# Four transposes of quantized codes as 16 bit halves, one hidden row per bank, and new step tables, in a chained four layer kernel on one Trainium2 core

## What is computed

```python
def _act_quant(x):
    scale = 127.0 / clip(max(abs(x), axis=-1), 1e-05)
    return clip(round(x * scale), -128, 127) / scale
def _bitlinear(x, w, nw):            # w is ternary times a scale
    xn = x * rsqrt(mean(square(x)) + 1e-08) * nw
    return act_quant(xn) @ weight_quant(w).T
# layer 0, for each element
mx = layernorm(x) * (1 + sc_msa) + s_msa
i, f, g = bitlinear(mx, wi), sigmoid(bitlinear(mx, wf)), bitlinear(mx, wg)
o = scan over tokens: h = f * h + silu(i) * (1 - f)
x = x + g_msa * bitlinear(rmsnorm(o) * silu(g), wo)
m = layernorm(x) * (1 + sc_mlp) + s_mlp
x = x + g_mlp * bitlinear(silu(gate) * y, wm2)    # gate, y = bitlinear(m, wm1)
# layer 1, for each element: a pre map, a fold over four tokens, a merge map,
# and y = gelu(h @ ffn_w1 + b) @ ffn_w2 + x with a hidden width of 1024
```

## Time and profile before

| what | value |
|---|---|
| timed runs, median (lowest to highest of 3) | 2154.37 us (2153.43 to 2154.45) |
| the profiled execution's own time | 2156.48 us |
| its span, first to last instruction | 2154.3 us |
| busy PE, DVE, ACT, POOL | 1839.9, 1328.7, 1121.0, 568.9 us |
| mean granted TensorE clock | 0.913 |

### The profile page before, as it was taken

The page is one execution under the profiler, slowest core; times in us unless marked ns, Lnnn a source line. Parts: engine busy times, 40 slices in busy tenths (PEclk is TensorE's granted clock), DMA queues, the critical chain, the costliest instruction groups (busy, mean ns, idle before and its releaser), DMA issues. The chain is left out here.

```text
span 2154.3 us, 26196 instructions
## 1 busy us (share of the span) xinstructions
PE 1839.9 (85%) x8728; PEld 1104.3 (51%) x8744; DVE 1328.7 (62%) x2922; ACT 1121.0 (52%) x2127; POOL 568.9 (26%) x775
## 2 busy tenths in 40 slices
PE   2355779999999996589899999999999856899998
PEld 1133557677766674133454545454544445567666
DVE  5757698878876516668786868677774114332331
ACT  6556588888776521046756575666666400221221
POOL 0256565567445213000010101010101100323322
PEclk9656699999999997589999999999999977999999
DMA  9400000000000003220203021111200020000000
GB/s 373 127 33 8 18 18 1 18 18 14 1 13 11 3 1 98 52 59 5 63 3 64 7 59 26 40 34 32 53 14 3 6 96 1 3 18 10 20 10 20
DMA packets 88312, 78.20 MB, mean 36 GB/s; under 512 B 9969, under 2 KB 82123, under 8 KB 87923
## 3 DMA queue, kind: packets, MB, share of 16 engines
q1 hardware_dynamic: 88080, 76.50, 12.9%
q10 hardware_dynamic: 98, 0.03, 0.0%
HBM read 46.67 MB, written 4.27 MB: 24 GB/s over the span
## 5 line engine op out<-in xcount | busy, mean ns | idle before, releaser
L1896 DVE TENSOR_REDUCE l_small<-l_psum 128x1 f32<-128x512 f32 x512 | 329.5, 684 | 137.2 <-PE l_psum L1843 132.3
L1655 ACT ACTIVATE l_prob<-l_psum 128x512 f32<-128x512 f32 x512 | 286.4, 596 | 230.0 <-PE l_psum L1713 226.7
L1843 PE MATMUL l_psum<-l_kT,l_qT 96*128 96x512 bf16 x512 | 192.2, 412 | 27.1 <-DMA l_kT<-l_early 12.1
L1713 PE MATMUL l_psum<-l_qT,l_kT 99*128 99x512 bf16 x512 | 175.6, 388 | 16.0 <-ACT l_prob L1655 14.3
L1639 POOL TENSOR_TENSOR k_x_res<-k_x_res,l_add 128x256 f32<-128x256 f32 x32 | 23.3, 727 | 469.9 <-DVE l_add L1940 469.9
L1722 PE MATMUL l_psum<-l_prob,l_v 128*32 128x512 f32 x1024 | 138.1, 612 | 0.2
L1843 PEld LDWEIGHTS l_psum<-l_kT,l_qT 96*128 96x128 bf16 x512 | 49.6, 98 | 171.1 <-DVE l_small L1896 117.9
L1787 PE MATMUL l_psum<-l_w,l_gu 128*128 128x256 f32 x512 | 134.8, 392 | 0.7 <-ACT l_gu L1671 0.7
L94 PE MATMUL l_psum<-l_hT,l_w_f 128*128 128x512 f32 x256 | 120.0, 597 | 5.7 <-ACT l_gu L1013 5.7
L94 PE MATMUL l_psum<-l_hT,l_w 128*128 128x512 f32 x256 | 116.8, 606 | 8.6 <-ACT l_hT L2250 8.6
L94 PE MATMUL l_psum<-l_turned_over,l_w 128*128 128x512 f32 x256 | 120.5, 597 | 4.2 <-ACT l_gu L1671 4.2
(11 more groups left out here) (389 smaller groups left out, 3891.5 us busy)
## 6 DMA issues: line engine op xcount, KB each, us to landing
su_raw<-in_L_cond_wa SPq DMA_DIRECT2D x6, 1536.0 KB, 21.9
l_qT<-l_early SPq DMA_DIRECT2D x32, 192.0 KB, 3.6
l_kT<-l_early SPq DMA_DIRECT2D x32, 192.0 KB, 3.3
k_x_res<-in_x SPq DMA_DIRECT2D x1, 4096.0 KB
l_w<-in_L_cond_W SPq DMA_DIRECT2D x4, 1024.0 KB, 12.5
l_qT<-l_early SPq DMA_DIRECT2D x32, 128.0 KB, 3.1
l_kT<-l_early SPq DMA_DIRECT2D x32, 128.0 KB, 3.0
out<-k_x_res SPq DMA_DIRECT2D x8, 512.0 KB, 2.9
```

The lines of the kernel that those rows point to most:

```text
L1655: act.activation(prob[:, s % 2, j, :], psum[:, 2 + n % 2, :], ACT.Exp, scale=float(HD) ** -0.5).then_inc(exp_ready.sem, 1)
L1713: pe.matmul(psum[:, 2 + n % 2, :], kT[e % 2][:, head, tok(s % T)], qT[e % 2][:, head, :], start=True, stop=True).then_inc(st_ready.sem, 1)
L1843: pe.matmul(psum[:, n % 2, :], qT[e % 2][0:SROWS, n // T, tok(n % T)], kT[e % 2][0:SROWS, n // T, :], start=True, stop=True).then_inc(s_re ...
L1896: dve.tensor_reduce(mx[:, n % T, n // T:n // T + 1], psum[:, n % 2, :], AX.X, ALU.max).then_inc(max_ready.sem, 1)
```

## The change

The code is now made with bias ROUND + CODE, CODE = 16384.0. The low 16 bits of the f32 word are then 16384 plus the code. `low(a)` views an f32 tile as bf16 and takes every second element, the low half. The turns of the stages xq, xoq, xq2 and hq read this view as weights, with step 2, against a bf16 identity `identb`, which POOL makes once. They write bf16 into PSUM, where a bank then holds 1024 columns. DVE reads the bank as uint16 (`codes_in`), subtracts CODE and writes bf16 as before. The turns of fi, o, turn and turn2 stay in f32.

The hidden row of 1024 now fits one bank: `hq` has four parts of 8 blocks, always in bank 4, `qhT` four parts of 1024 columns, and `y2` always goes to bank 5. The six blocks of `xq` fit bank 0. Five scratch tiles `junk` become bf16. The five tables are replaced; PE has 78 entries in place of 82, DVE 85 in place of 89.

```diff
+CODE = 16384.0
...
 SP_TURN = (
-    ("load_gate", 0, -70), ("load_mlp", 0, -70), ("load_norm", 0, -67), ("load_style", 0, -71))
+    ("load_style", 0, -113), ("load_norm", 0, -110), ("load_mlp", 0, -112), ("load_gate", 0, -111))
...
 PE_TURN = (
-    ("f1", 4, -1), ("pre", 1, 0), ("xq2", 0, 1), ("proj", 2, 2), ("xq2", 1, 1), ("gate", 0, 1), ("f1", 5, -1), ("up", 0, 1), ("xq", 3, 2),
-    ("gate", 1, 1), ("up", 1, 1), ("gate", 2, 1), ("dots", 0, 0), ("proj", 3, 2), ("up", 2, 1), ("gate", 3, 1), ("merge", 0, 0), ("up", 3, 1),
-    ("gate", 4, 1), ("fi", 0, 2), ("up", 4, 1), ("gate", 5, 1), ("fi", 1, 2), ("up", 5, 1), ("gate", 6, 1), ("f1", 6, -1), ("up", 6, 1),
-    ("gate", 7, 1), ("fi", 2, 2), ("fi", 3, 2), ("up", 7, 1), ("merge", 1, 0), ("f1", 7, -1), ("o", 0, 2), ("o", 1, 2), ("merge", 2, 0), ("o", 2, 2),
-    ("o", 3, 2), ("f2", 0, -1), ("f2", 1, -1), ("hq", 0, 1), ("hq", 1, 1), ("merge", 3, 0), ("f2", 2, -1), ("setup", 0, 7), ("y2", 0, 1),
-    ("f2", 3, -1), ("xoq", 0, 2), ("hq", 2, 1), ("hq", 3, 1), ("xoq", 1, 2), ("yo", 0, 2), ("xoq", 2, 2), ("f2", 4, -1), ("yo", 1, 2), ("xoq", 3, 2),
-    ("y2", 1, 1), ("yo", 2, 2), ("hq", 4, 1), ("hq", 5, 1), ("xq", 0, 3), ("yo", 3, 2), ("turn2", 0, 0), ("y2", 2, 1), ("hq", 6, 1), ("proj", 0, 3),
-    ("hq", 7, 1), ("f2", 5, -1), ("y2", 3, 1), ("turn2", 1, 0), ("xq", 1, 3), ("f2", 6, -1), ("proj", 1, 3), ("f2", 7, -1), ("f1", 0, 0),
-    ("xq", 2, 3), ("f1", 1, 0), ("turn", 0, 1), ("f1", 2, 0), ("turn", 1, 1), ("f1", 3, 0), ("pre", 0, 1))
+    ("up", 6, -1), ("f1", 1, -3), ("up", 7, -1), ("merge", 2, -2), ("o", 3, 0), ("f1", 2, -3), ("f1", 3, -3), ("f1", 4, -3), ("hq", 0, -1),
+    ("merge", 3, -2), ("hq", 1, -1), ("y2", 0, -1), ("f1", 5, -3), ("xoq", 0, 0), ("xoq", 1, 0), ("hq", 2, -1), ("yo", 0, 0), ("xoq", 2, 0),
+    ("y2", 1, -1), ("yo", 1, 0), ("xoq", 3, 0), ("f1", 6, -3), ("yo", 2, 0), ("xq", 0, 1), ("y2", 2, -1), ("yo", 3, 0), ("hq", 3, -1), ("f1", 7, -3),
+    ("proj", 0, 1), ("y2", 3, -1), ("turn2", 0, -2), ("f2", 0, -3), ("xq", 1, 1), ("f2", 1, -3), ("proj", 1, 1), ("turn2", 1, -2), ("f2", 2, -3),
+    ("xq", 2, 1), ("f2", 3, -3), ("proj", 2, 1), ("turn", 0, -1), ("f2", 4, -3), ("xq", 3, 1), ("turn", 1, -1), ("f2", 5, -3), ("pre", 0, -1),
+    ("proj", 3, 1), ("f2", 6, -3), ("fi", 0, 1), ("pre", 1, -1), ("xq2", 0, 0), ("fi", 1, 1), ("xq2", 1, 0), ("setup", 0, 48), ("fi", 2, 1),
+    ("gate", 0, 0), ("fi", 3, 1), ("up", 0, 0), ("f2", 7, -3), ("gate", 1, 0), ("f1", 0, -2), ("dots", 0, -1), ("up", 1, 0), ("gate", 2, 0),
+    ("merge", 0, -1), ("gate", 3, 0), ("up", 2, 0), ("o", 0, 1), ("o", 1, 1), ("gate", 4, 0), ("up", 3, 0), ("o", 2, 1), ("gate", 5, 0),
+    ("up", 4, 0), ("merge", 1, -1), ("gate", 6, 0), ("up", 5, 0), ("gate", 7, 0))
...
+        def low(a):
+
+            return a.bitcast(BF16).rearrange("p (n a) -> p n a", a=2)[:, :, 0]
+
+        def halves(a):
+            return psum[:, a, :].bitcast(BF16)
+
+        def codes_in(a, n):
+            return psum[:, a, :].bitcast(U16)[:, 0:n]
...
+                gp.tensor_copy(identb[:], ident[:]).then_inc(identb_ready, 1)
...
                         for j in range(3 * KD):
-                            last = turn(nc, two_banks(0)[:, tok(j)], xw[:, t, j // KD, tok(j % KD)], ident[:])
+                            last = turn(nc, halves(0)[:, tok(j)], low(xw[:, t, j // KD, tok(j % KD)]), identb[:])
...
-                        i, c = t // 2, t % 2
-                        pe.wait_ge(hq_ready.sem, hq_ready.at(e, i + 1))
-                        if i and c:
-                            pe.wait_ge(add2_ready.sem, add2_ready.at(e, i))
-                        elif i:
-                            pe.wait_ge(qhT_ready.sem, qhT_ready.at(e, 2 * i))
-                        for k in range(T):
-                            last = turn(nc, psum[:, 4 + (3 * i + c) % 2, tok(k)], h[:, i, tok(c * T + k)], ident[:])
+                        pe.wait_ge(hq_ready.sem, hq_ready.at(e, t + 1))
+                        if t:
+                            pe.wait_ge(qhT_ready.sem, qhT_ready.at(e, t))
+                        for k in range(KF):
+                            last = turn(nc, halves(4)[:, tok(k)], low(h[:, t, tok(k)]), identb[:])
                         last.then_inc(h_turned.sem, 1)
                     elif stage == "y2":
-                        pe.wait_ge(qhT_ready.sem, qhT_ready.at(e, 2 * t + 2))
-                        mm(nc, psum[:, 4 + (3 * t + 2) % 2, 0:D], [(qhT[:, t % 2, k, :], w_m2[:, k, :]) for k in range(KF)]).then_inc(y2_ready.sem, 1)
+                        pe.wait_ge(qhT_ready.sem, qhT_ready.at(e, t + 1))
+                        if t:
+                            pe.wait_ge(add2_ready.sem, add2_ready.at(e, t))
+                        mm(nc, psum[:, 5, 0:D], [(qhT[:, t % 2, k, :], w_m2[:, k, :]) for k in range(KF)]).then_inc(y2_ready.sem, 1)
...
-                        V.tensor_scalar(qhT[:, i % 2, c * T:(c + 1) * T, :].rearrange("p a n -> p (a n)"), psum[:, 4 + (3 * i + c) % 2, :], ROUND, None,
+                        V.tensor_scalar(qhT[:, t % 2, :, :].rearrange("p a n -> p (a n)"), codes_in(4, KF * P), CODE, None,
                                         ALU.subtract).then_inc(qhT_ready.sem, 1)
```

More of the change, by code:

```diff
@@ L16 @@
 F32 = mybir.dt.float32
+U16 = mybir.dt.uint16
 BF16 = mybir.dt.bfloat16
@@ L673, in layers01 @@
         gsq = z2
-        junk = [sb(f"junk{i}", [P, D]) for i in range(5)]
+        junk = [sb(f"junk{i}", [P, D], BF16) for i in range(5)]
         junk_h = sb("junk_h", [P, FF])
+        identb = sb("identb", [P, P], BF16)
         flat_gu = gu[:].rearrange("p a b -> p (a b)")
@@ L918, in _ @@
                         for j in range(3):
-                            last = ac.activation(xw[:, t, j, :], xw[:, t, j, :], ACT.Copy, bias=ROUND, scale=qs[e % 2][:, t, j:j + 1])
+                            last = ac.activation(xw[:, t, j, :], xw[:, t, j, :], ACT.Copy, bias=ROUND + CODE, scale=qs[e % 2][:, t, j:j + 1])
                         last.then_inc(xq_ready.sem, 1)
@@ L941, in _ @@
                         act.wait_ge(qso_ready.sem, qso_ready.at(e, 1))
-                        ac.activation(xo[:, t, :], xo[:, t, :], ACT.Copy, bias=ROUND, scale=qso[:, t:t + 1]).then_inc(xoq_ready.sem, 1)
+                        ac.activation(xo[:, t, :], xo[:, t, :], ACT.Copy, bias=ROUND + CODE, scale=qso[:, t:t + 1]).then_inc(xoq_ready.sem, 1)
                     elif stage == "ssq2":
@@ L949, in _ @@
                         act.wait_ge(qs2_ready.sem, qs2_ready.at(e, 1))
-                        ac.activation(mx2[:, t, :], mx2[:, t, :], ACT.Copy, bias=ROUND, scale=qs2[:, t:t + 1]).then_inc(xq2_ready.sem, 1)
+                        ac.activation(mx2[:, t, :], mx2[:, t, :], ACT.Copy, bias=ROUND + CODE, scale=qs2[:, t:t + 1]).then_inc(xq2_ready.sem, 1)
                     elif stage == "silu":
@@ L962, in _ @@
                         act.wait_ge(qsh_ready.sem, qsh_ready.at(e, 1))
-                        ac.activation(h[:, t, :], h[:, t, :], ACT.Copy, bias=ROUND, scale=qsh[:, t:t + 1]).then_inc(hq_ready.sem, 1)
+                        ac.activation(h[:, t, :], h[:, t, :], ACT.Copy, bias=ROUND + CODE, scale=qsh[:, t:t + 1]).then_inc(hq_ready.sem, 1)
                     elif stage == "setup":
@@ L1059, in _ @@
                         for k in range(KD):
-                            last = turn(nc, psum[:, t % 2, tok(k)], xo[:, t, tok(k)], ident[:])
+                            last = turn(nc, halves(t % 2)[:, tok(k)], low(xo[:, t, tok(k)]), identb[:])
                         last.then_inc(xo_turned.sem, 1)
@@ L1070, in _ @@
                         if e and t == 0:
-                            pe.wait_ge(qhT_ready.sem, qhT_ready.at(e - 1, 2 * T))
+                            pe.wait_ge(qhT_ready.sem, qhT_ready.at(e - 1, T))
                         elif e:
@@ L1075, in _ @@
                             for k in range(KD):
-                                last = turn(nc, psum[:, 4 + t, tok(KD * i + k)], mx2[:, 2 * t + i, tok(k)], ident[:])
+                                last = turn(nc, halves(4 + t)[:, tok(KD * i + k)], low(mx2[:, 2 * t + i, tok(k)]), identb[:])
                         last.then_inc(turned2.sem, 1)
@@ L1262, in _ @@
                             dve.wait_ge(yo_ready.sem, yo_ready.at(e, t - 1))
-                        V.tensor_scalar(qoT[:, t % 2, :, :].rearrange("p a n -> p (a n)"), psum[:, t % 2, 0:D], ROUND, None,
+                        V.tensor_scalar(qoT[:, t % 2, :, :].rearrange("p a n -> p (a n)"), codes_in(t % 2, D), CODE, None,
                                         ALU.subtract).then_inc(qoT_ready.sem, 1)
```

45 lines of the change are left out of this document (19 added, 26 removed), and 29 rows, old and new, of tables (ACT_TURN, DVE_TURN, POOL_TURN).

## The result

The changed kernel takes 2133.68 us (median, 2131.75 to 2135.23). The kernel before, timed beside it, takes 2153.9 us. The ratio is 0.9906 with an interval of 0.9889 to 0.9923. The profiled execution took 2134.47 us with a span of 2132.7 us. The forecast was 2130.0.

The account below looks back on a forecast made before the run. The prediction took PE to bound the middle and drain, with no engine full in the fill. Terms of -9.5, -6, -15.8, +6.6 and +0.3 gave -24.4 us from a span of 2154.3, a median of 2130.0, range 2111 to 2148.

Parts of the forecast that it names:

- the half slope of the moves: DVE's 16 bit moves from PSUM: fixed part plus half the f32 column cost, 5.4 us less of 60 per element.
- The first rival: PE turns: the 128 column, step 2 weight load sets the old 0.110 us pace; 2159 us in all, chance 7%.
- The term of 9.5: Fill to scan 2: cheaper turns and qT moves, a quarter hidden, save 3.2 us for each of three iterations.
- a fill 15 us off: Stated sign of a wrong prediction: the fill comes out 15 us away from forecast, scan 2 about 9 us earlier.
- a part that PE bounds: Middle, scans 3 to 7: PE is the bound, so each element's 3.95 us of cheaper turns shortens the iteration; -15.8 us.
- The third rival: Middle: a loop of ACT, PE and DVE passing tiles holds the iteration at 71, not 68.7; 2142 us, chance 17%.
- The +11 for f1 and f2: Drain: a pipeline some 0.4 iteration deeper moves about 11 us of PE's f1 and f2 work there from the fill.
- The identity: POOL makes identb ahead of its first root while ACT waits: 0.3 us added.
- One bank: Hidden row in one bank: waits counted as nothing; 2 us an iteration if the cover by other PE entries failed.
- The order of SP: SP puts mod_norm of element k + 3 behind style of k; it lands with 3 us to spare, counted as nothing.
- The two distances on PE: Between xq part 0 and f1 part 1 3.21 iterations before; to f2 part 0 now 4.12; used for the pipeline's depth.
- one to four other entries: PE's new table: entries between hq(t) and hq(t+1) that cover the wait for the qhT move.

Follow-up runs that it names:

- the halves alone: Kernel before, its tables and two half rows per hidden row kept, with only the 16 bit turns, moves, added CODE and bf16 junk: 2134.27 us, ratio 0.9907.
- the second profile of before: The kernel before, unchanged, run once more for a second trace: 2155.47 us.
- two further edits: Changed kernel without PE's wait for sg ahead of a block's turns and with 64 column dot products: 2126.71 us, ratio 0.9868.

## Why the prediction was right, and where it was not

**Prices.** The pace of 0.056 us per turn, the half slope of the moves and the weight load were all as taken. Eight loads and turns go by in 0.45 us. The first rival is out. The rule in the Trainium skill (TensorE: Matmul & The Clock Gate, section LDWEIGHTS), 107 ns for 128 columns, does not hold here as a pace, though the record of a single load lasts 102 ns.

The Trainium skill (VectorE: DVE Perf Modes, section "Why PSUM operands drop a tier") lets a 16 bit operand in PSUM run at up to twice the pace; its tier table has tensor_tensor with PSUM at one. The 682 and the 1217 ns for 1024 columns, uint16 from PSUM, agree with both.

**Terms.** Forecast, the halves alone (old order), and the change in all, in us:

| stretch | forecast | halves alone | change |
|---|---|---|---|
| to scan 2 | -9.5 | -10.6 | -28.5 |
| scan 2 to 3 | -6 | -0.9 | -0.2 |
| scans 3 to 7 | -15.8 | -4.8 | -9.4 |
| scan 7 to last x3 | +6.6 | -2.0 | +20.7 |
| to the last x3 | -24.7 | -18.4 | -17.5 |

*Fill.* The term of 9.5 is met by the halves alone. The -28.5 of the whole change isn't comparable: the scan was entry 23 of 89 in DVE's table and is now the first of 85, and a quarter of an iteration is 18 us. Corrected for it, fill and drain changed by -10.5 and +2.7. The prediction named a fill 15 us off as a sign of being wrong, and read by the scans that sign is met: scan 2 was forecast for about 266 us and came at 246.6, and the drain took 195.5 us, not 181. The scan's new place was in the tables, and I used it for the depth of the pipeline but not for the forecast of the scans. The correction of 18 us is an estimate from places in a table, so the split of fill and drain is no sharper than a few us.

*Middle.* This is the step that failed: "a part that PE bounds". A saving of 3.95 us per element arrived as 1.2 in the old order and 2.35 in the new. PE's busy time there fell by 2.9 an iteration (283.3 of 290.9 us to 271.7 of 281.5, with 17 us at the lower clock in both), and what was left of it went into idle time. The turns' other 1.0 us did not show even in the busy time. The third rival, another loop that holds the iteration at 71, had it right in place and nearly in size (70.4); it had 17%. Its total of 2142 was 8 us too slow. I took a busy share of 97% for proof of a bound. The page Perfetto Trace Analysis of the Trainium skill, section Identifying the Most-Contended Engine, says that matmul busy share is no good measure of how close a kernel is to roofline, since pipelined instructions look smaller in the trace. It doesn't speak of which engine sets the pace, so it would not have caught this error.

*Whole stage.* The windows show how far PE's saving went, before and then after:

```profile
88.00:815.00 727.00, 615.39 (x3012) 433.75 (x3028) 511.64 (x1053) 475.23 (x1143) 375.72 (x516) 0.88 0.06 18
```
```profile
88.00:798.00 710.00, 591.94 (x3009) 400.59 (x3028) 474.48 (x1022) 459.09 (x1134) 374.64 (x519) 0.87 0.06 18
```

576 turns at 0.055 us are 31.7 us; PE's busy time fell by 23.5 and its idle time rose by 6.4. Part of the difference went to other groups that got slower, above all the two merges, from 38.7 and 35.4 to 41.3 and 39.1 us. In the old order these two rose by only 1.7 together, and by 2.0 in the second profile of before; so most of the rise goes with the new order, in which they stand where the lower clock falls.

*Drain.* The +11 for f1 and f2 that move later was too much. The first f1 starts at 317.90 us instead of 307.01, so the deeper order is real. Corrected for the scan's place, the drain of the changed kernel is 4.7 us longer than with the halves in the old order, and its middle 4.6 us shorter. Some of that drain is chance of the clock: it has 13.7 us at the lower level, that of the first profile of before 10.2 and of the second 17.1, and against the second the corrected drain is 0.6 us shorter. The order's cost and gain cancel, and with them two errors of my sum: the middle was 12.2 us too good (scan 2 to 7), the drain some 4 too bad.

*Rest.* The identity was given 0.3; ACT's first wait for POOL is 5.27 us as in the earlier trace rows, so it costs nothing. One bank was given 0 and measured 0 to 3. The order of SP was given 3 us to spare; POOL waited 0.94 us for one of the four `mod_norm` of the middle, so that margin was just used up. The two distances on PE, 3.21 and 4.12 iterations, come out of the tables as 3.20 and 4.10; nothing changes by it. The text says "one to four other entries" between two `hq` on PE; between parts 2 and 3 there are ten, which only adds cover.

*Total.* The stage fell short of the sum by 7.2 us: 12.2 in the middle, less 3.9 in the drain and 1.0 in the fill. Against the second profile of before it fell short by 4.6, and the median by 3.7. The forecast was right by its prices and its fill; its middle stood on a bound that wasn't there, and the oversized drain covered a third of that, which was luck.

## What to carry to other kernels

A busy share of 97% doesn't show that an engine sets the pace: add some microseconds of work to it and see whether the iteration grows by as much. Here 1.8 us of turns gave 0.4. Compare the granted clock of the two traces before reading the difference: here it had taken back part of the added work. Ahead of a change to in-order tables, follow the chain of waits back until it meets the same instruction one iteration earlier, and look first for what the change takes from that loop. That this loop is what holds the iteration is a reading here; no run tested it. When an order and a cheaper operation come together, run the operation in the old order: here it carried the whole gain, and the new order paid only together with two further edits.

## What the runs showed of the hardware

A turn of 128x128 through every second 16 bit word of an f32 tile goes at 0.056 us, the pace of packed bf16 turns with 96 weight columns.

A subtraction of a constant from 1024 uint16 columns in PSUM takes 682 ns on DVE, and from a broadcast f32 column 1217 ns.

Thirty-two products with a single moving column, run without a gap, were followed by some 3 to 7 us at 1.2 GHz in each iteration of the middle. The same products with 64 columns took 273 to 275 ns each instead of 250 to 273, and in the traced run 6.8 of 17.0 us at the lower level were left there and none of 13.7 in the drain. Other runs of that kernel had a lower mean clock (0.914 to 0.918, against 0.921 in the traced one), so the edit need not end these dips in every run. The Trainium skill (TensorE: Matmul & The Clock Gate, section "HAM oscillation — how this bites in real kernels") has the clock fall behind waits of PE; here it fell with no wait before it, and the measurement decides.

The time at the lower clock differs between executions of the same kernel. Two traces of the kernel before have 10.2 and 17.1 us of it in the drain, and the drains take 174.8 and 178.1 us.
